# The bias behind the first norm moves from GpSimd to TensorE, and the step lists are laid out anew

## The chip, the cores and the metric

The kernel runs on one core of a Trainium2 chip. The metric is the device time of one execution in microseconds (us), the median of three runs. Five engines work side by side, each through its own list of instructions, and meet at semaphores: TensorE (PE in the profile; its weight loads are shown as PEld), VectorE (DVE), ScalarE (ACT), GpSimd (POOL) and SyncE (SP), which only issues transfers.

## The reference, cut to what matters

Input x is 16 batches of 512 tokens with 256 features. After a layer norm two branches run: an attention block with its own feed-forward layer, and a feed-forward layer with blockwise FP4 rounding, whose SiLU gates the first. The change sits in the attention block, behind the attention itself:

```
h   = _ln(x + attn_out, ln1_g, ln1_b)
ffn = gelu(h @ ffn_w1 + ffn_b1) @ ffn_w2 + ffn_b2
s   = _ln(h + ffn, ln2_g, ln2_b)
out = x0 + s * silu(fp4_ffn(x))
```

So the sum that enters the second norm is (x + attn_out, normed) * ln1_g + ln1_b + ffn_b2 + gelu(...) @ ffn_w2. The two rows ln1_b and ffn_b2 (256 numbers each) are the same for every token.

## The kernel before

Tokens lie on the 128 partitions, four groups of 128 tokens to a batch (T = 4). One batch is worked at a time, but its work is staggered: while the attention of batch b runs (`sc` scores, `pv` products with the values, `mx` row maxima for the other half batch, `proj` and `v` projections of batch b + 1, and the FP4 layer `gu`, `tr`, `dn`), the feed-forward part of batch b - 1 runs too (`cT`, `out`, `hT`, `f1`, `f2`, and the norms `ln1`, `ln2`). All this is cut into some 150 to 200 steps, and the order in which each of the five engines takes its steps is written out by hand in the table `ORDER`: a part `head` (setup and batch 0), a part `mid` that is repeated for batches 1 to 14, and a part `end` (batch 15 and the feed-forward part that is left over, `tail`). In `head` and `end` a step has its stretch in front (`pre:`, `pro:`, `first:`, `last:`, `tail:`). The engines do not reorder anything: a step that waits holds up all that stands behind it on its engine.

PSUM banks are given out in the order of TensorE's steps: banks 0 and 1 to `sc`, 6 and 7 in turn to `xT`, `proj`, `v`, `mx` and `mT`, and 2 to 5 in turn to all others. A step that reuses a bank waits for the engine that read it last, so a `mx` step waits for VectorE to be done with the `mx` step two before.

Steps that the change touches or that the prediction speaks of:

- `f2.t` on TensorE (L774 to L782): the second layer of the feed-forward part for 128 tokens, eight float32 products of 256 columns summed in one bank. In the trace each float32 product is two MATMUL rows (L781), a bfloat16 product is one.
- `f2.t` on VectorE (L1180 to L1183) adds the bank to `y2`.
- `lnb1` on GpSimd (L1273 to L1280): `y2 = hY * ln1_g`, then `y2 = y2 + (ffn_b2 + ln1_b)`, each 128x1024 per batch, in the tail in halves of 128x512. VectorE's `f2.t` waits for the second (event `g_hb2`).
- `xnb` on GpSimd (L1234 to L1246): xn + out_b, which VectorE's `out` adds; in batch 0 it first makes the sum of the two bias rows (L1238). SyncE's `xload` (L480 to L483) fetches the next batch into `xn` only when it is done (event `g_xnb`), and VectorE's `norm` of that batch waits for the load.
- `mul` on GpSimd (L1212), the elementwise product of the past score blocks, three instructions per head pair; `hq` and `hr`, the FP4 rounding of the gate branch (L1256, L1262, L1264); `tr` on TensorE (L723) waits for the last of them.
- in the setup, `wm` on GpSimd (L1440, L1442), `ws` and `wr` on VectorE (L1514 to L1528): FP4 rounding of the three weight matrices; `ws.2` needs the load `c2` (L1391, in_w_down). `soft` (L1572 to L1577) is the last step of the kernel-mask setup.
- `busy` on TensorE (L1672): products of no use in the setup.

Of the kernel before, what the change touches and what calls it, by code (L numbers as in the profile page):

```python
# [56 lines left out]
class Event:  # L57
# [5 lines left out]
    def wait(self, eng, b, k=None):  # L63

        if isinstance(b, int) and b < 0:
# [17 lines left out]
            pre:half pre:rs.0 pre:rs.1 pre:ones pre:iota pre:rs.2 pre:wm.0.0 pro:projm.0 pro:projm.1 pre:rs.3 pre:rs.4  # L83
            pro:projm.2 pre:rs.5 pre:rs.6 pre:rs.7 pre:rs.8 pre:rs.9 pre:rs.10 pre:wm.0.1 pre:rs.11 pre:rs.12 pre:wm.1.0
            pre:rs.13 pre:rs.14 pre:rs.15 pre:wm.1.1 pro:xq first:xnb pre:wm.2.0 pro:xr pre:wm.2.1 first:projm.0
            first:xq first:projm.1 first:projm.2 first:xr first:mul.0 first:mul.1 first:hq.0 first:mul.2 first:hr.0
# [16 lines left out]
            first:mx.1.3.0 first:muld.0.1 first:mx.1.3.1 first:silu.0.0 first:silu.0.1 first:mx.1.3.2 first:muld.1.0
            first:mx.1.3.3 first:hq.0 first:muld.1.1 first:v.0 first:mx.1.3.4 first:muld.2.0 first:mfin.1 first:v.1
            first:muld.2.1 first:hr.0 pre:pad first:silu.1.0 first:muld.3.0 first:muld.3.1 first:silu.1.1 first:silu.2.0
            pre:join first:muld.4.0 first:hq.1 first:muld.4.1 first:silu.2.1 first:hq.2 first:muld.5.0 first:hr.1
            first:muld.5.1 first:ctxt.0 first:mx.0.0.0 first:ctxt.1 first:mx.0.0.1 first:muld.6.0 first:dn.0
            first:mx.0.0.2 first:mx.0.0.3 first:mx.0.0.4 first:muld.6.1 first:silu.3.0 first:hr.2 first:silu.3.1
            first:mx.0.1.0 first:muld.7.0 first:mx.0.1.1 first:mx.0.1.2 first:mx.0.1.3 first:mx.0.1.4 first:muld.7.1
            first:hq.3 first:mx.0.2.0 first:mx.0.2.1 first:mx.0.2.2 first:mx.0.2.3 first:dn.1 first:mx.0.2.4  # L110
            first:mx.0.3.0 first:hr.3 first:mx.0.3.1 first:mx.0.3.2 first:ctxt.2 first:mx.0.3.3 first:mx.0.3.4
            first:dn.2 first:mfin.0 first:ctxt.3 first:dn.3
        """,
        tensor="""
            pre:arg.0 pre:arg.1 pre:arg.2 pre:arg.3 pre:sum.0 pre:arg.4 pre:arg.5 pre:arg.6 pre:sum.1 pre:sum.2
            pre:arg.7 pro:xT.0 pre:arg.8 pro:xT.1 pre:arg.9 pro:proj.0 pro:proj.1 pre:arg.10 pro:proj.2 pre:sum.3
            pre:sum.4 pre:arg.11 pro:v.0 pre:busy.0 pre:sum.5 pre:arg.12 pro:v.1 pre:sum.6 pre:sum.7 pre:busy.1
            pre:busy.2 pre:busy.3 pre:sum.8 pre:arg.13 pro:mx.0.0.0 pre:busy.4 pre:busy.5 pro:mx.0.0.1 pro:mx.0.0.2
            pre:sum.9 pro:mx.0.0.3 pro:mx.0.0.4 pro:mx.0.1.0 pre:sum.10 pre:busy.6 pro:mx.0.1.1 pro:mx.0.1.2 pre:sum.11
            pre:busy.7 pro:mx.0.1.3 pro:mx.0.1.4 pre:busy.8 pre:busy.9 pre:sum.12 pro:mx.0.2.0 pro:mx.0.2.1 pre:busy.10  # L120
            pre:busy.11 pre:busy.12 pre:busy.13 pro:mx.0.2.2 pre:busy.14 pro:mx.0.2.3 pre:busy.15 pro:mx.0.2.4
            pre:busy.16 pro:mx.0.3.0 pre:busy.17 pro:mx.0.3.1 pro:mx.0.3.2 pre:busy.18 pre:sum.13 pro:mx.0.3.3
            pre:sum.14 pro:mx.0.3.4 pre:sum.15 pre:sum.16 pre:busy.19 pre:sum.17 pre:poolT first:mx.1.0.0 pre:arg.14
            pre:mod first:mx.1.0.1 pre:gl pre:stat first:mx.1.0.2 first:mx.1.0.3 pro:mT.0 pre:arg.15 first:mx.1.0.4
            pre:busy.20 pre:wide first:mx.1.1.0 first:mx.1.1.1 pre:wt.0 first:mx.1.1.2 pre:kern pre:busy.21 pre:wt.1
            pre:wt.2 first:xT.0 pre:wt.3 first:xT.1 pre:wt.4 first:mx.1.1.3 pre:wt.5 pre:wt.6 first:mx.1.1.4 pre:wt.7
# [1678 lines left out]
```

## Time and profile before

| | us |
|---|---|
| median of three runs (1857.62 to 1858.73) | 1857.88 |
| the profiled execution, its own time | 1861.0 |
| its span, first to last instruction | 1859.2 |
| TensorE busy in the span | 1799.9 (97%) |
| VectorE, GpSimd, ScalarE busy | 1504.4 (81%), 1214.8 (65%), 1022.1 (55%) |
| mean granted TensorE clock | 0.991 |

Busy time is the time in which an engine has at least one instruction under way. TensorE's matmuls are pipelined: the mean length of one (380 ns for 256 float32 columns) is longer than the distance from its start to the next one's start, and it is that distance which counts when an engine is full.

### The profile page before, as it was taken

How to read it: one execution, taken by the hardware profiler on the slowest of the kernel's cores; microseconds unless marked ns; L12 is line 12 of the kernel's file. 1: busy time of each engine (PE TensorE's matmuls, PEld its weight loads, DVE VectorE, ACT ScalarE, POOL GpSimd, SP SyncE). 2: the span in 40 equal slices, each digit the busy share in tenths (PEclk: the TensorE clock that was granted, in tenths of full speed). 3: DMA queues.
4: the chain of work that ended last, by engine and by line, in shares of the span. 5: the costliest groups of instructions: out<-in, count | busy, mean ns of one | idle time of the engine just before them, and what ended most of it. 6: DMA issues, size and time to landing. Idle time of an engine off the chain costs nothing.

```text
span 1859.2 us, 37329 instructions
## 1 busy us (share of the span) xinstructions
PE 1799.9 (97%) x12687; PEld 1299.1 (70%) x12693; DVE 1504.4 (81%) x4977; ACT 1022.1 (55%) x2062; POOL 1214.8 (65%) x843
## 2 busy tenths in 40 slices
PE   8978999999999999999999999999999999999997
PEld 3335677777777777777777777777777777777766
DVE  6888889787888978788888978788897878888762
ACT  5535464655647465554736565564746555473642
POOL 3345677666758667675867767675875767586573
PEclk9989999999999999999999999999999999999999
DMA  6614242333323233333314233332323333331211
GB/s 189 200 43 109 56 140 79 100 113 89 114 80 106 74 102 116 96 102 100 113 52 139 80 100 110 93 113 70 113 78 100 113 93 109 100 112 49 65 59 35
DMA packets 146791, 181.44 MB, mean 98 GB/s; under 512 B 20605, under 2 KB 101630, under 8 KB 146596
## 3 DMA queue, kind: packets, MB, share of 16 engines
q1 hardware_dynamic: 146602, 179.05, 32.8%
q8 instruction: 103, 1.69, 0.4%
q14 instruction: 86, 0.70, 0.1%
HBM read 142.53 MB, written 36.47 MB: 96 GB/s over the span
## 4 chain that ended last, share of the span: by engine, by line
PE 58%; issue 20%; DVE 16%; POOL 4%; ACT 1%; DMA 1%; POOLq 0%; DVEq 0%; SPq 0%; ACTq 0%
PE ps L772 12%; PE ps L781 12%; PE ps L713 9%; PE ps L686 4%; PE ps L636 4%; PE ps L606 3%; PE ps L670 3%; PE ps L623 3%; DVE nmax L1068 2%; PE ps L666 2%; DVE Pr L1098 2%; DVE ps L1068 2%; POOL slot L1262 1%; PE ps L1598 1%; DVE y L1003 1%
## 5 line engine op out<-in xcount | busy, mean ns | idle before, releaser
L1068 DVE CUSTOM_DVE_ANT_0 ps<-ps,future 128x512 f32<-128x512 f32 (+3 forms) x1024 | 476.9, 516 | 62.6 <-issue 60.3
L1212 POOL TENSOR_TENSOR Pr<-Pr,Tz 128x768 f32<-128x768 f32 (+2 forms) x384 | 481.8, 1283 | 66.8 <-ACT Pr L854 65.4
L854 ACT ACTIVATE Pr<-ps 128x384 f32<-128x384 f32 x512 | 242.9, 487 | 210.3 <-PE ps L670 207.5
L772 PE MATMUL ps<-catT,w 128*128 128x256 f32 x1024 | 242.2, 382 | 1.1 <-ACT catT L919 1.1
L636 PE MATMUL ps<-KS,QS 108*128 108x512 bf16 (+3 forms) x1024 | 223.3, 301 | 10.7 <-DVE nmax L1068 4.1
L781 PE MATMUL ps<-w,gT 128*128 128x256 f32 x1024 | 232.3, 380 | 0.9 <-ACT gT L944 0.9
L781 PEld LDWEIGHTS ps<-w,gT 128*128 128x128 f32 x1024 | 190.8, 190 | 25.6 <-ACT gT L944 1.3
L772 PEld LDWEIGHTS ps<-catT,w 128*128 128x128 f32 x1024 | 188.4, 190 | 27.7 <-ACT catT L919 1.3
L1098 DVE SCALAR_TENSOR_TENSOR Pr<-ps,Tz 128x512 f32<-128x512 f32 x256 | 176.1, 688 | 31.5 <-ACT ps L843 26.3
L1272 POOL TENSOR_TENSOR rstd<-ve,minus_half 128x4 f32<-128x4 f32 (+1 forms) x34 | 33.5, 986 | 243.5 <-DVE ve L997 243.5
L1262 POOL TENSOR_TENSOR slot<-slot 128x704 f32<-128x704 f32 x64 | 107.6, 1681 | 120.5 <-DVE slot L972 120.5
L843 ACT ACTIVATE ps<-ps 128x512 f32<-128x512 f32 x256 | 150.5, 588 | 61.9 <-PE ps L666 61.6
L730 PE MATMUL ps<-wdT,hqT 128*128 128x256 f32 x768 | 178.8, 382 | 0.0
L713 PE MATMUL ps<-wgT,xqT 128*128 128x352 f32 x512 | 175.3, 465 | 1.1 <-ACT xqT L874 1.1
L713 PE MATMUL ps<-wuT,xqT 128*128 128x352 f32 x512 | 173.8, 462 | 0.0
L670 PE MATMUL ps<-QS,KS 112*128 112x384 bf16 (+2 forms) x768 | 160.6, 273 | 7.2 <-DVE Pr L1098 3.6
L730 PEld LDWEIGHTS ps<-wdT,hqT 128*128 128x128 f32 x768 | 141.6, 190 | 20.3 <-ACT hqT L893 2.3
L686 PE MATMUL ps<-Pr,v_cur 128*17 128x128 f32 (+2 forms) x3584 | 151.1, 319 | 0.0
L636 PEld LDWEIGHTS ps<-KS,QS 108*128 108x128 bf16 x1024 | 88.7, 98 | 87.7 <-DVE nmax L1068 30.6
L1068 DVE DVE_READ_ACCUMULATOR2_ANT nmax<- 128x1 f32 x1024 | 144.2, 141 | 0.0
L713 PEld LDWEIGHTS ps<-wuT,xqT 128*128 128x128 f32 x512 | 96.1, 190 | 58.7 <-ACT gT L944 7.4
L1256 POOL TENSOR_TENSOR slot<-slot,sc_h 128x704 f32<-128x704 f32 x64 | 95.5, 1492 | 59.8 <-PE ps L723 37.0
(251 smaller groups left out, 3351.2 us busy)
## 6 DMA issues: line engine op xcount, KB each, us to landing
Tz<-kernel_rows SPq DMA_DIRECT2D x256, 256.0 KB, 3.8
KS<-k_parts SPq DMA_DIRECT2D x32, 384.0 KB
QS<-q_parts SPq DMA_DIRECT2D x64, 192.0 KB
hY<-in_x SPq DMA_DIRECT2D x19, 512.0 KB, 5.2
xn<-in_x SPq DMA_DIRECT2D x17, 512.0 KB, 5.2
out<-y SPq DMA_DIRECT2D x15, 512.0 KB, 3.0
xnT<-in_x_t SPq DMA_DIRECT2D x14, 512.0 KB, 6.7
q_parts<-q_sp SPq DMA_DIRECT2D x16, 384.0 KB, 2.9
```

What stands on the lines that cost most here:

```text
L636: ins = mm(o, QS[0:KROWS, 2 * p + e, it * P:(it + 1) * P], KS[0:KROWS, p, 0:n], start=True, stop=True)
L670: ins = mm(dst[:, at:at + PAST[j]], KS[0:SROWS, p, j * P:(j + 1) * P], rhs[:, S - 1:P * (j + 1) - 1:-1], start=True, stop=True)
L686: ins = mm(dst[32 * hh:32 * hh + HD + 1, to:to + n], v_cur[:, j, 4 * g + hh, :], rhs[:, n - 1::-1], start=i == 0, stop=i == len(pieces) - 1)
L713: ins = mm(dst[:, 0:IH], xqT[:, c, t * P:(t + 1) * P], wt[:, c, f * IH:(f + 1) * IH], start=c == 0, stop=c == KD - 1)
L730: ins = mm(dst[:, 0:D], hqT[:, c * P:(c + 1) * P], wdT[:, c, :], start=c == 0, stop=c == KI - 1)
L772: ins = mm(dst[:, i * n:(i + 1) * n], w1[:, c, f * P:(f + 1) * P], catT[:, c, hf * n:(hf + 1) * n], start=c == 0, stop=c == KD - 1)
L781: ins = mm(dst[:, 0:D], gT[:, f, at:at + P], w2[:, f, :], start=f == 0, stop=f == KF - 1)
L843: inc(af(src, src, ACT.Exp), "a_exp")
L854: inc(af(Pr[:, p % 4, e, at:at + wd], src[:, 0:wd], ACT.Exp), "a_exp")
L1068: ins = v.tensor_tensor_reduce(o, o, future[:, S - n:S], -1.0, 3e38, ALU.add, ALU.min, nmax[:, 2 * pl + e, it:it + 1])
L1098: v.scalar_tensor_tensor(blocks(Pr[:, p % 4, e, 0:S]), blocks(ps[:, SC_BANKS[n % len(SC_BANKS)], :]), 3e38, near, ALU.min, ALU.mult).then_ ...
L1212: ins = g.tensor_tensor(a, a, Tz[:, p % 2, :, P * j:P * j + PAST[j]], ALU.mult)
```

## The change

Two things are done. First, GpSimd's second instruction of `lnb1` goes (the addition of `ffn_b2 + ln1_b` to all tokens), with the event `g_hg` between the two. In its place every `f2.t` step on TensorE gets a ninth product into the same bank: 96 rows deep, 128 wide, 256 columns, bfloat16. Its stationary side `bias_pick` is zero but for rows 0, 32 and 64, which are one; its moving side `bias_rows` holds in these rows the bias row cut into three bfloat16 parts, high, middle and low, whose sum is the float32 row. Both lie in the tile of `ln1_b`, no longer needed as such. The parts are made once, by ten more GpSimd instructions ahead of the first `xnb`.

Second, the table `ORDER` is laid out anew for all five engines in all three parts. The lines that compute, cut to the core (of `ORDER`, one line as an example):

```diff
-            ln1 mul.0 lnb1 xnb mul.1 hq.0 xt mul.2 hr.0 projm.0 hq.1 projm.1 mul.3 projm.2 hr.1 xq mul.4 hq.2 hr.2 mul.5
+            ln1 mul.0 xnb lnb1 mul.1 hq.0 xt mul.2 hr.0 hq.1 projm.0 mul.3 projm.1 projm.2 hr.1 xq mul.4 hq.2 hr.2 mul.5
...
+        bias_split = row["ln1_b"][:].bitcast(BF16)
+        bias_rows, bias_pick = bias_split[0:96, 0:D], bias_split[0:96, D:D + P]
...
                     for f in range(KF):
                         at = (t % 2) * P
-                        ins = mm(dst[:, 0:D], gT[:, f, at:at + P], w2[:, f, :], start=f == 0, stop=f == KF - 1)
-                    inc(ins, "pe_f2")
+                        mm(dst[:, 0:D], gT[:, f, at:at + P], w2[:, f, :], start=f == 0, stop=False)
+                    if b == 1 and t == 0:
+                        pe.wait_ge(L["row_sum"], 11)
+                    inc(mm(dst[:, 0:D], bias_pick, bias_rows, start=False, stop=True), "pe_f2")
...
                         pool.wait_ge(L["row_sum"], 1)
+                        r = row["ffn_b2"]
+                        g.memset(bias_pick, 0.0).then_inc(L["row_sum"], 1)
+                        pool.wait_ge(L["row_sum"], 2)
+                        for i in range(3):
+                            g.memset(bias_pick[32 * i:32 * i + 1, :], 1.0).then_inc(L["row_sum"], 1)
+                            pool.wait_ge(L["row_sum"], 3 + i)
+                        g.tensor_copy(bias_rows, r[0:96]).then_inc(L["row_sum"], 1)
+                        pool.wait_ge(L["row_sum"], 6)
+                        g.tensor_tensor(r[0:96], r[0:96], bias_rows, ALU.subtract).then_inc(L["row_sum"], 1)
+                        pool.wait_ge(L["row_sum"], 7)
+                        for i in (1, 2):
+                            g.tensor_copy(bias_rows[32 * i:32 * i + 32, :], r[32 * i:32 * i + 32]).then_inc(L["row_sum"], 1)
+                            pool.wait_ge(L["row_sum"], 7 + i)
+                        g.tensor_tensor(r[64:96], r[64:96], bias_rows[64:96, :], ALU.subtract).then_inc(L["row_sum"], 1)
+                        pool.wait_ge(L["row_sum"], 10)
+                        g.tensor_copy(bias_rows[64:96, :], r[64:96]).then_inc(L["row_sum"], 1)
+                        pool.wait_ge(L["row_sum"], 11)
...
-                    inc(g.tensor_tensor(y2[:, tt, :], hY[:, tt, :], wide("ln1_g"), ALU.mult), "g_hg")
-                    E["g_hg"].wait(pool, b - 1, hf)
-                    inc(g.tensor_tensor(y2[:, tt, :], y2[:, tt, :], wide("ffn_b2"), ALU.add), "g_hb2")
+                    inc(g.tensor_tensor(y2[:, tt, :], hY[:, tt, :], wide("ln1_g"), ALU.mult), "g_hb2")
```

Three places of the lists, each before and after. In these rows a tile that is written stands left of the arrow; `ps` is PSUM.

TensorE in a batch of the repeated part, around the first `f2` step, before:

```order
L670 MATMUL ps<-QS,KS 128x384
L636 MATMUL ps<-KS,QS 128x256 x2
L781 MATMUL ps<-w,gT 128x256 x8
L670 MATMUL ps<-QS,KS 128x256
L670 MATMUL ps<-QS,KS 128x128
L666 MATMUL ps<-QS,KS 128x128 x4
L644 MATMUL ps<-ident_bf,sh_sp 16x128 x4
L606 MATMUL ps<-xnT,cq 128x512 x2
```

The same place after the change (lines are three to six numbers further down; L784 is the old L781, L787 the new product, which names only the one tile that holds both its operands):

```order
L673 MATMUL ps<-QS,KS 128x384
L639 MATMUL ps<-KS,QS 128x256 x2
L784 MATMUL ps<-w,gT 128x256 x8
L787 MATMUL ps<-row_ln_b 128x256
L673 MATMUL ps<-QS,KS 128x256
L673 MATMUL ps<-QS,KS 128x128
L669 MATMUL ps<-QS,KS 128x128 x4
L647 MATMUL ps<-ident_bf,sh_sp 16x128 x4
L609 MATMUL ps<-xnT,cq 128x512 x2
```

The steps here stand in the same order; each `f2` has one bfloat16 product of 256 columns more.

GpSimd in the setup, from the bias row's sum to the rounding of the third weight matrix, before (L1238 makes the sum, L1245 is `xnb`, L1442, L1440 and L1442 are `wm.2`):

```order
L1238 TENSOR_TENSOR row_ffn_b<-row_ffn_b,row_ln_b 128x256 [waits pro_w_rest,pro_stat]
L1245 TENSOR_TENSOR xnb<-xn,row_out_b 128x1024 [waits v_norm,pro_row_sum]
L1442 TENSOR_TENSOR gT<-gT,gs_old 128x1536 [waits pro_wq]
L1227 TENSOR_TENSOR catT<-catT,sc_x 128x1024 [waits v_xq]
L1440 TENSOR_TENSOR gT<-gT,slot 128x768 [waits pro_wq]
L1440 TENSOR_TENSOR gT<-gT,hqT 128x768
L1442 TENSOR_TENSOR gT<-gT,gs_old 128x1536 [waits pro_wpool]
```

and after:

```order
L1243 TENSOR_TENSOR row_ffn_b<-row_ffn_b,row_ln_b 128x256 [waits pro_w_rest,pro_stat]
L1246 MEMSET row_ln_b 96x128 [waits pro_row_sum]
L1249 MEMSET row_ln_b 1x128 [waits pro_row_sum] x3
L1251 CAST row_ln_b<-row_ffn_b 96x256 [waits pro_row_sum]
L1253 TENSOR_TENSOR row_ffn_b<-row_ffn_b,row_ln_b 96x256 [waits pro_row_sum]
L1256 CAST row_ln_b<-row_ffn_b 32x256 [waits pro_row_sum] x2
L1258 TENSOR_TENSOR row_ffn_b<-row_ffn_b,row_ln_b 32x256 [waits pro_row_sum]
L1260 CAST row_ln_b<-row_ffn_b 32x256 [waits pro_row_sum]
L1267 TENSOR_TENSOR xnb<-xn,row_out_b 128x1024 [waits v_norm,pro_row_sum]
L1462 TENSOR_TENSOR gT<-gT,gs_old 128x1536 [waits pro_wq]
L1460 TENSOR_TENSOR gT<-gT,slot 128x768 [waits pro_wq]
L1460 TENSOR_TENSOR gT<-gT,hqT 128x768
```

Ten small instructions (the rows with x3 and x2 counted as such) stand between the sum and `xnb`, and the second scaling of the rounded input (L1227) no longer stands between the two parts of `wm.2`.

SyncE in the setup, from the last load of the weights to the first transfer of the masks' shifts, before:

```order
L1391 DMA gT<-in_w_down 128x2x704
L1403 DMA stat_rows<-xnb 64x128 [waits pro_statc]
L1403 DMA stat_rows<-xnb 64x128
L483 DMA xn<-in_x 128x4x256 [waits g_xnb,g_xs]
L537 DMA shift_parts<-sh_T 16x512 [waits a_mT]
L543 DMA QS<-shift_parts 2x4x512 [waits d_shw0]
L543 DMA QS<-shift_parts 2x4x512
```

and after:

```order
L1423 DMA stat_rows<-xnb 64x128 [waits pro_statc]
L1423 DMA stat_rows<-xnb 64x128
L540 DMA shift_parts<-sh_T 16x512 [waits a_mT]
L546 DMA QS<-shift_parts 2x4x512 [waits d_shw0]
L546 DMA QS<-shift_parts 2x4x512
L1411 DMA gT<-in_w_down 128x2x704
L486 DMA xn<-in_x 128x4x256 [waits g_xnb,g_xs]
```

The load of `in_w_down` stood ahead of two waits and now stands behind three, and the load of `xn` behind it.

## Rows read from the trace of the kernel before

**Rows 1.** The page, part 1: busy us, share of the span, instructions.

```profile
PE 1799.9 (97%) x12687; PEld 1299.1 (70%) x12693; DVE 1504.4 (81%) x4977; ACT 1022.1 (55%) x2062; POOL 1214.8 (65%) x843
```

**Rows 2.** Windows: stretch, its length, then busy us, instructions by engine, clock, DMA.

```profile
100.00:150.00 50.00, 34.34 (x184) 17.18 (x185) 45.26 (x112) 21.15 (x55) 19.13 (x9) 0.80 0.11 21
329.04:1712.33 1383.29, 1373.56 (x9987) 1021.69 (x9985) 1150.29 (x3823) 786.15 (x1535) 953.72 (x651) 1.00 0.33 98
```

**Rows 3.** Timeline, TensorE in one batch: start us, us, engine, line, what, count.

```profile
1005.75 0.33 PE L670 MATMUL ps<-QS,KS 112*128 112x256 bf16 x2
1005.92 0.60 PE L694 MATMUL ps<-ident,ctxT 128*128 128x128 f32 x4
...
1007.38 3.62 PE L781 MATMUL ps<-w,gT 128*128 128x256 f32 x16
1010.83 0.33 PE L670 MATMUL ps<-QS,KS 112*128 112x256 bf16 x2
```

**Rows 4.** Timeline, TensorE in the setup, where the rows in use change.

```profile
96.88 0.39 PE L636 MATMUL ps<-KS,QS 108*128 108x512 bf16 x1
97.20 1.12 PE L1611 MATMUL ps<-ctxT,Tz 6*128 6x512 f32 x2
98.25 0.62 PE L1629 MATMUL ps<-pooledT,gs 128*128 128x16 f32 x4
```

**Rows 5.** Timeline over one batch's seam, TensorE.

```profile
1181.05 0.38 PE L636 MATMUL ps<-KS,QS 108*128 108x256 bf16 x2
1181.71 0.88 PE L723 MATMUL ps<-ident,slot 128*128 128x128 f32 x6 [0.28 <-POOL slot L1264]
...
1193.11 0.33 PE L670 MATMUL ps<-QS,KS 112*128 112x256 bf16 x2
1193.45 0.40 PE L666 MATMUL ps<-QS,KS 112*128 112x128 bf16 x4
1194.02 0.34 PE L670 MATMUL ps<-QS,KS 112*128 112x384 bf16 x1 [0.18 <-ACT Pr L854]
```

**Rows 6.** Lines by form: count, busy us, mean ns, idle us ahead.

```profile
L1280 POOL TENSOR_TENSOR y<-y,row_ffn_b 128x1024 f32<-128x1024 f32 x15 | 35.4, 2357 | 1.2
```

**Rows 7.** Timeline, GpSimd in the setup.

```profile
13.09 0.24 POOL L1419 MEMSET ident_bf<- 128x128 bf16 x1
...
110.05 0.98 POOL L1238 TENSOR_TENSOR row_ffn_b<-row_ffn_b,row_ln_b 128x256 f32<-128x256 f32 x1 [7.51 <-DMA stat_rows<-xnb]
111.11 3.21 POOL L1245 TENSOR_TENSOR xnb<-xn,row_out_b 128x1024 f32<-128x1024 f32 x1
121.45 2.81 POOL L1442 TENSOR_TENSOR gT<-gT,gs_old 128x1536 f32<-128x1536 f32 x1 [7.13 <-DVE gs_old L1519]
```

**Rows 8.** Timeline, SyncE and VectorE in the setup.

```profile
114.39 0.38 SPq L483 DMA_DIRECT2D xn<-in_x  x1
114.82 0.50 SPq L537 DMA_DIRECT2D shift_parts<-sh_T  x1
118.47 1.42 SPq L543 DMA_DIRECT2D QS<-shift_parts  x2
...
118.11 1.75 DVE L1514 TENSOR_REDUCE gs_old<-gT 128x96 f32<-128x1536 f32 x1
125.30 1.22 DVE L972 TENSOR_TENSOR catT<-catT,hY 128x1024 f32<-128x1024 f32 x1
```

**Rows 9.** DMA issues between 60 and 150 us: KB each, us to landing.

```profile
gT<-in_w_down SPq DMA_DIRECT2D x1, 704.0 KB, 9.1
xn<-in_x SPq DMA_DIRECT2D x1, 512.0 KB, 3.7
```

**Rows 10.** The chain in the last batch (first row); timeline of the tail.

```profile
1729.23 0.96 ACT gs_old L905
...
1824.58 1.27 POOL L1280 TENSOR_TENSOR y<-y,row_ffn_b 128x512 f32<-128x512 f32 x1
1833.70 0.42 DVE L1183 TENSOR_TENSOR y<-ps,y 128x256 f32<-128x256 f32 x1 [9.92 <-PE ps L781]
```

More of the change, by code:

```diff
@@ L82 @@
         gpsimd="""
[L83 to L86, printed above, removed]
+            pre:half pre:iota pre:rs.0 pre:rs.1 pre:rs.2 pre:wm.0.0 pro:projm.0 pre:rs.3 pro:projm.1 pre:rs.4
+            pro:projm.2 pre:ones pre:rs.5 pre:rs.6 pre:rs.7 pre:rs.8 pre:rs.9 pre:rs.10 pre:wm.0.1 pre:rs.11 pre:rs.12
+            pre:wm.1.0 pre:rs.13 pre:rs.14 pre:rs.15 pre:wm.1.1 pro:xq first:xnb pre:wm.2.0 pre:wm.2.1 pro:xr first:xq
+            first:projm.0 first:projm.1 first:xr first:projm.2 first:mul.0 first:mul.1 first:hq.0 first:mul.2 first:hr.0
             first:mul.3 first:hq.1 first:mul.4 first:hr.1 first:hq.2 first:mul.5 first:hr.2 first:mul.6 first:hq.3
@@ L103 @@
[L103 to L112, printed above, removed]
+            pre:modT first:mx.1.0.0 first:mx.1.0.1 pre:fr.14 pre:peak first:mx.1.0.2 first:mx.1.0.3 pre:topk
@@ new lines @@
+            first:mx.1.0.4 first:mx.1.1.0 pre:fr.15 pre:kw first:mx.1.1.1 first:mx.1.1.2 pro:xr pre:ws.2 pro:xr2
+            first:norm pre:wr.2 pre:soft first:mx.1.1.3 first:mx.1.1.4 pre:join first:xq first:mx.1.2.0 first:proj.0
+            first:mx.1.2.1 first:proj.1 first:xr first:proj.2 first:mx.1.2.2 first:xr2 first:muld.0.0 first:mx.1.2.3
+            first:mx.1.2.4 first:mx.1.3.0 first:muld.0.1 first:mx.1.3.1 first:silu.0.0 first:muld.1.0 first:silu.0.1
+            first:mx.1.3.2 first:mx.1.3.3 first:hq.0 first:muld.1.1 first:mx.1.3.4 first:silu.1.0 first:v.0
@@ L117 @@
[L117 to L126, printed above, removed]
@@ new lines @@
+            pre:busy.11 pro:mx.0.2.1 pro:mx.0.2.2 pre:busy.12 pre:busy.13 pro:mx.0.2.3 pre:busy.14 pro:mx.0.2.4
+            pre:busy.15 pro:mx.0.3.0 pro:mx.0.3.1 pre:busy.16 pre:busy.17 pre:busy.18 pro:mx.0.3.2 pro:mx.0.3.3
+            pre:sum.13 pre:sum.14 pre:sum.15 pro:mx.0.3.4 pre:sum.16 pre:sum.17 first:mx.1.0.0 first:mx.1.0.1 pre:arg.14
+            pre:stat pre:busy.19 pre:poolT pre:arg.15 pre:mod pre:gl first:mx.1.0.2 first:mx.1.0.3 pro:mT.0
+            first:mx.1.0.4 pre:busy.20 first:mx.1.1.0 pre:wide first:mx.1.1.1 first:mx.1.1.2 pre:kern pre:wt.0
@@ L161 @@
+            first:dn.2 first:tr.3.0 first:tr.3.1 first:mT.0 first:dn.3
         """,
@@ L204 @@
         sync="""
-            last:T.0 last:load.1 last:T.1 last:T.2 last:T.3 last:mio.1 last:T.4 last:T.5 last:T.6 last:T.7 last:fin
+            last:T.0 last:load.1 last:T.1 last:T.2 last:T.3 last:T.4 last:mio.1 last:T.5 last:T.6 last:T.7 last:fin
             tail:xr tail:fin.0 tail:fin.1
@@ L208 @@
         gpsimd="""
-            last:ln1 last:hq.0 last:mul.0 last:hr.0 last:mul.1 last:hq.1 last:lnb1 last:mul.2 last:xnb last:hr.1
-            last:mul.3 last:hq.2 last:mul.4 last:hr.2 last:mul.5 last:hq.3 last:hr.3 last:mul.6 last:mul.7 last:ln2
-            last:fin tail:ln1.0 tail:ln1.1 tail:lnb1.0 tail:lnb1.1 tail:ln2.0 tail:fin.0 tail:ln2.1 tail:fin.1
+            last:ln1 last:hq.0 last:mul.0 last:hr.0 last:xnb last:mul.1 last:lnb1 last:mul.2 last:hq.1 last:mul.3
+            last:hr.1 last:hq.2 last:mul.4 last:hr.2 last:mul.5 last:hq.3 last:hr.3 last:mul.6 last:mul.7 last:ln2
@@ L223 @@
-            tail:ln1.1 tail:lnc1.1 last:dn.3 tail:f2.0 tail:f2.1 tail:ln2.0 tail:lnc2.0 tail:lnb2.0 tail:f2.2 tail:f2.3
-            tail:ln2.1 tail:lnc2.1 tail:lnb2.1
+            last:silu.0.0 last:out.0 last:out.1 last:muld.0.0 last:ln1 last:silu.0.1 last:muld.0.1 last:lnc1 last:hq.0
+            last:silu.1.0 last:muld.1.0 last:mx.1.0.0 last:mx.1.0.1 last:mx.1.0.2 last:muld.1.1 last:silu.1.1
+            last:mx.1.0.3 last:hr.0 last:mx.1.0.4 last:mx.1.1.0 last:mx.1.1.1 last:muld.2.0 last:mx.1.1.2 last:muld.2.1
@@ L256 @@
+            tail:f1.1.0 tail:f1.1.1 tail:f1.1.2 tail:f1.1.3
         """,
```

222 lines of the change are left out of this document (115 added, 107 removed).

## Prediction

> **What bounds the kernel.** I read the page's busy times first: TensorE is busy for 97% of the span, GpSimd, which the change relieves, for 65% [rows 1]. A mean over stages proves little, so the windows come next. From the first transposes of batch 1's rounded tokens to those of batch 14 (thirteen equal stretches, 106.4 us each) TensorE is busy for 1373.6 of 1383.3 us, VectorE for 83%, GpSimd for 69%; the setup from 100 to 150 us is another matter, there VectorE is busy for 45.3 of 50 us and TensorE for 34.3, at a clock of 0.80 [rows 2]. In the repeated part, then, whatever is added to TensorE lengthens the batch, and whatever is taken from GpSimd is worth only what TensorE waits because of it. In the setup it is the other way round.
>
> Busy time hides short waits, since the ends of matmuls are modelled. So I read the timeline start to start. The 16 rows of one `f2` go from 1007.38 to 1010.83, 0.216 us each [rows 3], with no room between. At a seam between batches I find real waits: the two 256-column products at 1181.05 need 0.22 us, but the next step starts 0.66 us later, a wait of 0.44 us for the last rounding on GpSimd (`tr.3.0`); at 1193.11 and 1193.45 a step of 0.16 and one of 0.22 us are followed at 0.34 and 0.57 us, another 0.53 us, for ScalarE's exponentials [rows 5]. Going through one batch in this way I count about 2.2 us of such waits, in ten places. They recur alike in each batch. That is all that a new order could give back in a batch.
>
> **The change, part by part.**
>
> *The ninth product.* Four `f2` steps per batch, 16 batches: 64 products of 256 bfloat16 columns. The nearest rows: a 256- and a 128-column bfloat16 product together take 0.17 us (1005.75 to 1005.92) [rows 3], so two thirds, 0.11 us, for 256 columns. Those use 112 of the array's rows, this one 96. It stands behind float32 products of 128 rows and 128 columns, as the `sc` steps often do, and the trace shows no loss there: behind the `f2` at 1007.38 the next row starts on time. 64 x 0.11 = 7.0 us. Ends: 128 columns' worth, 0.055 us each, 3.5 us; and 0.11 plus a loss at the change of shape on both sides, 0.30 us each, 19 us (second rival). I take 7.0, and all of it on the path, since the waits listed above hang on TensorE's own progress: `mx` steps wait for VectorE to finish a `mx` that TensorE has delivered just before, `tr.3.0` for a chain that starts behind `dn.1`. None stands behind an `f2` and could swallow its lengthening.
>
> *GpSimd's addition.* 15 of 2.357 us [rows 6] and two halves of 1.27 us in the tail [rows 10], 37.9 us of GpSimd's time. Who waits for it? VectorE's `f2`, which in the tail starts at 1833.70, when the last addition has been done since 1825.85 [rows 10]; in a batch the distance is larger. What stands behind it on GpSimd is `xnb` and `mul.1`. They come 2.4 us sooner, but the next point where TensorE waits for GpSimd is `tr.3.0`, 80 us further on, and there GpSimd itself waited before it for VectorE's rounding `hr.3`. So the gain is nothing; at the other end, if all of the 0.44 us went in 14 batches, 6 us.
>
> *The new order of the repeated part.* I laid the two lists side by side at each of the ten waits. For `sc.0.3` and `sc.0.4` ScalarE's copy `vcopy` has been moved from ahead of `sc.0.1` to ahead of `cT`; but `sc.0.4` reuses the bank of `sc.0.2`, which TensorE delivers at 1193.44 (1193.11 and its own 0.33) and ScalarE then reads; it started at 1194.02 [rows 5], and can't start much sooner in either order. In the first quarter `mx.1.1.0` gets its bank some 0.15 us sooner, but `f1.0.0` behind it waits for ScalarE's `hT` as before. From `dn.1` on, where four of the waits lie (0.06 to 0.45 us), TensorE's steps are the same. In the third quarter the `mx` steps are pulled forward by one, which lets VectorE start sooner but also brings each closer to the one whose bank it takes; by my sums they keep 0.1 to 0.9 us in hand. So I take 0 for the 14 batches, with 0.3 us per batch either way, 4 us.
>
> *The setup.* Ten small GpSimd instructions stand between the bias sum and `xnb`. Bounds: 0.24 us, as a memset of 128x128, and 0.98 us, as an addition of 128x256 [rows 7]. Four memsets near the first and six others at 0.5 to 1.0 us, with some 0.1 us between them: 5 to 8 us, I take 6.3. Behind `xnb` (ended 114.3) GpSimd was idle for 7.13 us, until VectorE had the scales of the third weight matrix [rows 7]; this covers it, barely. But `xload` also waits for `xnb`: it was issued at 114.39 and takes 3.7 us [rows 8, 9]; 6.3 us later it lands at 124.4. VectorE wanted it behind the scales, which GpSimd took up at 121.45 [rows 7]. In the new order the two roundings `xr2`, two instructions of 1.22 us [rows 8], stand ahead of it, so it is wanted at 123.9: 0.5 us late, less what the statistics arrive sooner. Further, the load of `in_w_down` stood ahead of everything, and now stands behind the shifts' transfers. The first of them landed 3.65 us after it was issued (114.82 to 118.47) [rows 8]; from a start near 108.5, my estimate from the order of ScalarE's steps, and with 1.4 us for the next two [rows 8], the weight load is issued at about 113.6. It took 9.1 us when many loads were under way [rows 9]; alone, scaled from 512 KB in 3.7 us [rows 9], 5.1 us, so it lands at 118.7 to 122.7, and VectorE wants it at 118.11 [rows 8]. VectorE has no idle time from there on. I take 0.6 us for this and 0.1 for `xload`; with the rest of the setup's new order, of which I can work out little, the bounds are -4 and +5 us.
>
> *The last batch.* ScalarE's copy `gs_old`, 0.96 us [rows 10], no longer stands directly ahead of the normalization that TensorE's `hT` waits for; an exponential of 0.48 us takes its place. I take -0.5 us.
>
> *Sum.* 7.0 + 0 + 0 + 0.7 - 0.5 = 7.2 us. The profiled execution took 1861.0 us, of which 1.8 us lie around the span of 1859.2 us; it becomes 1868.2. The median of the runs is 3.1 us lower than that execution, and the same sum on it gives 1857.9 + 7.2 = 1865.1 us.
>
> **The rivals.**
>
> *The waits go (the other side).* With GpSimd and VectorE less pressed, the new order could meet the banks in time: if half of the 2.2 us per batch goes, 14 x 1.1 = 15 us, against 7: 1850 us. For it speaks that all lists have been laid out anew around the lighter GpSimd; against it, that the waits I looked up are set by TensorE's own step and the one reader behind it, in both orders. It wins from 0.6 us per batch on.
>
> *A loss at each ninth product.* Where the rows in use change from 108 to 6 and back to 128, the trace shows losses: the 512-column product at 96.88 is followed after 0.32 instead of 0.22 us, and the two at 97.20 take 1.05 instead of 0.86 us [rows 4], so about 0.1 us each way. If 96 rows counted as a change of shape, 0.19 us x 64 = 12 us more, 1877 us. Against it: 108, 112 and 128 rows alternate everywhere without loss. 
>
> *The setup loses.* The weight load lands late by its long duration (4.6 us), and the small instructions take 8 us, so `xload` is late by 2: about 5 us more than I take, 1870 us.
>
> *The order gives a little.* Some 0.25 us per batch in 14 batches, 3.5 us: 1861.5 us.
>
> A second rule of the skill bears on the product's price: "TensorE: Matmul & The Clock Gate", Back-to-back issue gap, gives some 81 ns for 128 and 131 ns for 512 columns in a stream of weight loads and matmuls. By it, read between the two, 64 products would cost about 6 us. The rows of this kernel disagree for 512 columns (0.22 us), and the sum goes by them.
>
> **How the numbers follow.** Forecast 60%; the order gives a little 15%; the setup loses 10%; the waits go 10%; a loss at each product 5%. The range from 1859 to 1871 takes in the forecast with its own bounds (the 4 us of the order and the setup's, not both at their ends), the setup's loss and most of the small gain. A difference of 0.2%, 3.7 us, is about what a measurement of this kernel can tell from none: 1854.2 to 1861.6. Faster than that: 9%, nearly all from the first rival. Within: 16%, from half of the small gain and the forecast's lower edge. Slower: 75%.
>
> **What would show it.** In the profile after: 64 more bfloat16 matmuls of 96 rows, followed by the next row after 0.11 us; a batch of 106.8 us instead of 106.4; 38 us less on GpSimd, and longer idle stretches there. The wait of 0.44 us at `tr.3.0` and the 0.53 us at `sc.0.3` and `sc.0.4` are still there. In the setup, VectorE's fourth norm step behind `xr2` at about 124 us. I am wrong in the step on the order if a batch takes 106.4 us or less, in the price of the product if it takes 107.2 or more, and in the setup if batch 1 starts more than 3 us earlier or later than the sum says.

## The result, and the profile after

| | before | changed |
|---|---|---|
| median, us (5 runs each) | 1858.33 (1857.62 to 1860.96) | 1866.13 (1865.23 to 1869.89) |
| the profiled execution, its span | 1861.0, 1859.2 | 1869.89, 1868.1 |

The ratio is 1.0038, 95% interval 1.0027 to 1.0048: 7.1 us slower (5.0 to 8.9). The forecast was 1865.1 us. The profiled execution of the changed kernel is the longest of its five, so the profiled pair shows 8.9 us; 1.8 of these lie ahead of the repeated batches, nearly all in the setup, and I come back to them.

The page, part 1, of the changed kernel: TensorE has its 64 matmuls more than in [rows 1], GpSimd loses 12.8 us where I had said 38.

```profile
PE 1811.4 (97%) x12751; PEld 1307.4 (70%) x12757; DVE 1513.1 (81%) x4977; ACT 1017.8 (54%) x2064; POOL 1202.0 (64%) x836
```

Two windows of the changed kernel, columns as in [rows 2]: the thirteen repeated batches between the same two instructions as there, and what follows. These two are the first transposes of the rounded tokens of batch 2 and of batch 15, counted from 0 as in the lists; the prediction calls them batch 1's and batch 14's, and what it calls the start of batch 1 is the transposes of batch 0 (`pro:xqT`). No sum hangs on that.

```profile
330.82:1719.81 1388.99, 1378.49 (x10038) 1026.60 (x10037) 1155.51 (x3823) 779.49 (x1535) 939.73 (x638) 1.00 0.34 98
1719.81:1868.10 148.29, 132.65 (x890) 103.88 (x888) 82.12 (x250) 70.00 (x140) 71.78 (x54) 0.99 0.17 50
```

1388.99 against 1383.29 us [rows 2] is 5.70 us, or 13 x 4 x 0.11 us. From start to start, TensorE's timeline of one `f2` shows where they are: the ninth product (L787) starts at 1122.46, the next row at 1122.58.

```profile
1122.46 0.27 PE L787 MATMUL ps<-row_ln_b 96*128 96x256 bf16 x1
1122.58 0.33 PE L673 MATMUL ps<-QS,KS 112*128 112x256 bf16 x2
```

The seam between batches 9 and 10 answers to [rows 5]. The two `mx` products at 1186.73 are followed after 0.67 us (0.66 before); `sc.0.3` at 1198.97 is followed after 0.74 us where its four products take 0.22, so 0.52 us of waiting (0.53 before).

```profile
1186.73 0.38 PE L639 MATMUL ps<-KS,QS 108*128 108x256 bf16 x2
1187.40 0.87 PE L726 MATMUL ps<-ident,slot 128*128 128x128 f32 x6 [0.29 <-POOL slot L1286]
...
1198.80 0.33 PE L673 MATMUL ps<-QS,KS 112*128 112x256 bf16 x2
1198.97 0.39 PE L669 MATMUL ps<-QS,KS 112*128 112x128 bf16 x4
1199.71 0.34 PE L673 MATMUL ps<-QS,KS 112*128 112x384 bf16 x1 [0.36 <-ACT Pr L859]
```

So far the trace says: product at its price, order nothing. The experiments show that the second half of this is true only of the two together.

### The profile page after: what moved, and what is told of

It reads as the page before. It is cut to its first block, busy times and chain, and to the rows that moved or that the text cites. A ratio compares the mean times of both kernels' runs of the same rounds, so it can differ in the third digit from the quotient of the medians.

```text
span 1868.1 us, 37450 instructions
## 1 busy us (share of the span) xinstructions
PE 1811.4 (97%) x12751; PEld 1307.4 (70%) x12757; DVE 1513.1 (81%) x4977; ACT 1017.8 (54%) x2064; POOL 1202.0 (64%) x836
## 4 chain that ended last, share of the span: by engine, by line
PE 55%; issue 21%; DVE 18%; POOL 4%; ACT 1%; DMA 0%; POOLq 0%; DVEq 0%; SPq 0%; ACTq 0%
PE ps L775 11%; PE ps L784 11%; PE ps L716 9%; PE ps L639 4%; PE ps L689 4%; PE ps L609 3%; PE ps L673 3%; DVE nmax L1073 2%; PE ps L669 2%; DVE Pr L1103 2%; DVE ps L1073 2%; PE ps L626 1%; POOL slot L1284 1%; DVE y L1008 1%; DVE y L1016 1%
## 5 line engine op out<-in xcount | busy, mean ns | idle before, releaser
L784 PE MATMUL ps<-w,gT 128*128 128x256 f32 x1024 | 233.1, 381 | 0.9 <-ACT gT L949 0.9
L784 PEld LDWEIGHTS ps<-w,gT 128*128 128x128 f32 x1024 | 190.3, 190 | 26.4 <-ACT gT L949 1.3
L1278 POOL TENSOR_TENSOR slot<-slot,sc_h 128x704 f32<-128x704 f32 x64 | 101.3, 1583 | 78.3 <-DVE sc_h L966 47.0
```

What stands on the lines that cost most here:

```text
L784: mm(dst[:, 0:D], gT[:, f, at:at + P], w2[:, f, :], start=f == 0, stop=False)
```

## The experiments

Each kernel was timed in turns with the kernel before, whose median was then 1859.9 to 1860.7 us, some 2 us higher than above; so ratios are compared, not times. "Batch" is the median distance between the thirteen repeated batches in the one profiled execution: 106.34 us in the kernel before, 106.78 in the changed one. The mean is 0.1 us or less above it, but for three kernels that are named below.

### The product alone, the lists alone

Edit of the first: all three parts of `ORDER` as before, the rest as changed. Edit of the second: the other way round.

> The changed code with the step lists of the kernel before in all three parts: the ninth products alone. Theory (product at the price of its 256 rows, 64 x 0.11 us, nothing hidden; the lists pay about 1 us of their own in the setup): 1858.3 + 7.0 = 1865.3 us, that is 0.8 us under the changed kernel. Rival A (the lists carry the loss, the product hides in waits): near 1859 to 1861. Rival B (the new lists win something in the repeated batches and the product costs more than 0.11 us): above 1867, and the repeated batch over 106.85 us. Repeated batch by the theory: 106.34 + 0.44 = 106.78 us.

Measured: 1867.89 us against 1860.67, ratio 1.0036 (1.0023 to 1.0048), batch 106.79 us. The same as the changed kernel. Rival A falls by the time, and rival B by the batch, which is under its 106.85 us.

> The code of the kernel before (GpSimd adds the bias, eight products) with the new step lists in all three parts: the new order alone. Theory: 0 in the repeated batches (106.34 us each) and +1 to +2 us at the setup and the last batch: 1859.3 to 1860.3. Rival A (the order itself costs most of the 7.8 us): 1864 or more. Rival B (the order gives something that the product hides): under 1857.5, with a repeated batch under 106.2 us.

Measured: 1883.73 us, ratio 1.0118 (1.0103 to 1.0134). The theory is far off, the change in parts does not add up: product +6.7 us, lists +22, both together +7.1. The batch takes 107.84 us. Two of VectorE's rows, grouped by line, say where to look. They are the addition of epsilon to the variances (128x4 values, four on each partition), in this kernel and then in the changed one:

```profile
L998 DVE TENSOR_SCALAR ve<-mv 128x4 f32<-128x4 f32 (+1 forms) x34 | 25.6, 752 | 1.2
```

```profile
L1002 DVE TENSOR_SCALAR ve<-mv 128x4 f32<-128x4 f32 (+1 forms) x34 | 6.5, 192 | 1.2
```

### The ninth product left out, and issued twice

```diff
-                    inc(mm(dst[:, 0:D], bias_pick, bias_rows, start=False, stop=True), "pe_f2")
+                    inc(ins, "pe_f2")        # ins: the eighth product, with stop=True
```

> The changed kernel with its ninth product left out (the sum ends at the eighth f32 product, so the two biases are missing from the second layer); everything else as changed, the part rows are still made in the setup. Theory: 64 x 0.11 = 7.0 us less than the changed kernel, 1859.1 us, and it agrees with the kernel that has the new lists alone. Rival A (a wait moves into the gap): less than 4 us less, 1862 or more. Rival B (a shape change of 0.19 us at each product as well): 12 us or more less, under 1855.

Measured: 1883.27 us, ratio 1.0115 (1.0100 to 1.0130), batch 107.84. Taking 64 products out of the changed kernel makes it 14 us slower. It agrees with the kernel that has the lists alone, as expected, but both are on the far side of what any of the theories allowed. The timeline of one batch of this kernel, VectorE, GpSimd and then TensorE, shows the mechanism:

```profile
1274.61 1.63 DVE L1002 TENSOR_SCALAR ve<-mv 128x4 f32<-128x4 f32 x1
1276.16 0.56 DVE L1073 CUSTOM_DVE_ANT_0 ps<-ps,future 128x384 f32<-128x384 f32 x1
```

```profile
1274.40 1.81 POOL L1217 TENSOR_TENSOR Pr<-Pr,Tz 128x768 f32<-128x768 f32 x1 [0.29 <-ACT Pr L859]
```

```profile
1277.07 0.39 PE L639 MATMUL ps<-KS,QS 108*128 108x512 bf16 x1 [0.24 <-DVE nmax L1073]
1278.50 0.67 PE L626 MATMUL ps<-vw,xnT 128*128 128x256 f32 x2 [1.04 <-DVE nmax L1073]
```

GpSimd's product starts at 1274.40 and ends at 1276.21. VectorE's addition of 128x4 values starts at 1274.61, 0.20 us behind it, and ends at 1276.24, with it. It lasts 1.63 us; the next maxima are late by as much, and TensorE waits for them at `v.1`. In the changed kernel the same two instructions stand so:

```profile
1266.11 0.17 DVE L1002 TENSOR_SCALAR ve<-mv 128x4 f32<-128x4 f32 x1
```

```profile
1266.12 1.82 POOL L1217 TENSOR_TENSOR Pr<-Pr,Tz 128x768 f32<-128x768 f32 x1 [0.51 <-ACT Pr L859]
```

VectorE is ahead by 15 ns, and not held. In its thirteen repeated batches the lead is 4 to 15 ns, in the kernel without the product VectorE is behind by 193 to 207 ns, in the kernel before ahead by some 400. Between 4 ns ahead and 193 ns behind lies 1.5 us per batch. Where exactly the edge lies the runs do not show: one addition that the trace puts 2 ns behind (in the kernel with the setup's old lists, further down) was not held. The four products of a batch shift the two instructions by 0.2 us against each other with the old lists too: with the product alone the lead is 0.65 us. The Trainium skill's "SBUF — State Buffer", section "Who interferes with whom", has the rule: VectorE and GpSimd share one pair of ports, an exclusive lock for a whole instruction, taken by whichever issues first, and `tensor_scalar` is among the operations that can need it. This trace agrees: in the repeated batches the addition is held to within 0.03 us of the end of GpSimd's instruction where it is behind, and not where it is ahead.

> The changed kernel with the ninth product issued twice in each sum (the biases are added twice): 64 more bf16 products of the same kind, back to back with the first. Theory: each costs its 0.11 us again, 7.0 us more than the changed kernel: 1873.1 us, batch 107.22 us. Rival A (the first one pays for a change of type that the second does not): clearly less than what leaving out the first gives back. Rival B (products are partly covered by the waits of the batch): less than 4 us more.

Measured: 1873.85 us, ratio 1.0075 (1.0063 to 1.0088), against 1.0038 a further 0.37% or 6.9 us. Batch 107.2 us, 0.43 more; the second product starts 0.11 us behind the first. VectorE's lead grows to some 240 ns. The price is linear but for one of the thirteen batches. That one took 112.3 us, 5.1 more than the others (the mean is 107.6), and it shows how dear the edge is: a copy of 128x4 values starts 0.03 us behind GpSimd's product and lasts 1.80 us, the addition behind it is held as well, and TensorE waits twice for the maxima, 1.89 and 1.04 us. After these waits the clock granted to TensorE was 0.57 in the mean from 1057 to 1061 us, so for most of it at the lower of its two levels (1.2 instead of 2.4 GHz), and the eight rows of `v.1` took 3.31 us from start to start instead of 1.73. VectorE, GpSimd, then TensorE:

```profile
1052.45 1.80 DVE L998 COPY ve<-st 128x4 f32<-128x4 f32 x1
1054.57 0.90 DVE L1003 TENSOR_SCALAR ve<-mv 128x4 f32<-128x4 f32 x1
```

```profile
1052.42 3.71 POOL L1218 TENSOR_TENSOR Pr<-Pr,Tz 128x768 f32<-128x768 f32 x3
```

```profile
1056.31 0.39 PE L639 MATMUL ps<-KS,QS 108*128 108x512 bf16 x1 [1.89 <-DVE nmax L1074]
1057.74 3.48 PE L626 MATMUL ps<-vw,xnT 128*128 128x256 f32 x8 [1.04 <-DVE nmax L1074]
```

Why VectorE came late in that one batch I did not trace.

### The lists alone, without the collision

```diff
-        mv = sb("mv", [P, T, 2])
+        mv = sb("mv", [P, T, 3])                   # column 2 holds EPS
...
-                inc(v.tensor_scalar(ve[:, tt], mv[:, tt, 1], EPS, None, ALU.add), "v_ve")
+                inc(v.tensor_reduce(ve[:, tt], mv[:, tt, 1:3], AX.X, ALU.add), "v_ve")
```

> As the kernel with the new lists alone, but the one VectorE operation that was held there by GpSimd (the addition of the epsilon on 128x4 values, 1.63 us in the repeated batches against 0.17 us in the changed kernel) is a reduction over two columns instead, the second a constant column of epsilon; same place in the list, same values. Theory (the new lists put this operation 0.2 us behind the start of a 1.81 us GpSimd product, they share a port into SBUF, and the wait of 1.2 us of TensorE at v.1 is that): the operation takes about 0.2 us again, the wait at v.1 goes, batch 106.4 us or less instead of 107.84, total 1883.7 - 15 x 1.45 = 1862 us, range 1859 to 1864. Rival (the lists lose the 1.5 us by the order of the steps itself, the long operation only shows idle time): the batch stays above 107.5 us and the total above 1880.

Measured: 1864.00 us against 1860.49, ratio 1.0022 (1.0013 to 1.0030), batch 106.39. By the ratio that is 18 us less than with the scalar addition, and its time is the upper edge of what was expected. The two instructions stand as unluckily as before, VectorE's 0.20 us behind, and it takes 0.16 us:

```profile
1259.11 0.16 DVE L998 TENSOR_REDUCE ve<-mv 128x4 f32<-128x8 f32 x1
```

```profile
1258.91 1.82 POOL L1213 TENSOR_TENSOR Pr<-Pr,Tz 128x768 f32<-128x768 f32 x1 [0.28 <-ACT Pr L855]
```

That settles what costs the 1.5 us per batch: the held addition, since the order of the steps is the same in both kernels. That a shared port is what holds it is the page's account; the runs show who is held and for how long. The same page of the Trainium skill says of `tensor_reduce` on this chip that it never contends; the rows agree. What stays are 4 us by the ratio, and in the profiled execution 3.1 lie behind the repeated part (149.96 us from the window's end to the end, against 146.87). The kernel with the lists alone has the same (149.7); without GpSimd's addition and without the product it is 147.4. So the new order of the last batch loses some 2.5 us when GpSimd still has its addition to make, and fits the changed code only. Each is a figure of one execution.

> The changed kernel with the epsilon added by the two-column reduction instead of the scalar addition, as in the lists-alone kernel that lost its long operation. Theory (in the changed kernel this addition starts just ahead of GpSimd's product and is not held, 192 ns in the mean): nothing to remove, 1866.1 us within 2 us, batch 106.78 us. Rival (some of the change's loss is also such a collision): 1862 or less.

The same edit on the changed kernel. Measured: ratio 1.0045 (1.0032 to 1.0057), batch 106.77. Nothing to gain there, as expected.

### The product with 32 rows

```diff
-                    inc(mm(dst[:, 0:D], bias_pick, bias_rows, start=False, stop=True), "pe_f2")
+                    inc(mm(dst[:, 0:D], bias_pick[0:32], bias_rows[0:32], start=False, stop=True), "pe_f2")
```

> The changed kernel with only the first 32 rows in the ninth product (the high part of the bias alone; middle and low parts are left out). Theory: 32 rows lie behind a product of 128 rows as another shape of the array and lose what other products of 32 or 16 rows lose there, some 0.09 to 0.19 us each: 64 x 0.14 = 6 to 12 us more, 1872 to 1878 us. Rival (only the number of columns sets the price): 1866 us, a ninth product followed after 0.11 us as before.

Measured: 1882.18 us (2 runs), ratio 1.0120 (1.0100 to 1.0139), batch 107.63; the rival falls, and the time is above the theory's range. TensorE's timeline around one of them:

```profile
1233.15 0.59 PE L784 MATMUL ps<-w,gT 128*128 128x256 f32 x2
1233.68 0.28 PE L787 MATMUL ps<-row_ln_b 32*128 32x256 bf16 x1
1233.89 0.34 PE L673 MATMUL ps<-QS,KS 112*128 112x256 bf16 x2
```

The last row of the `f2` starts at 1233.37 (two rows from 1233.15, 0.22 apart) and is followed after 0.31 instead of 0.22 us; the ninth is followed after 0.21 instead of 0.11. So 0.2 us are lost on the two sides together, as [rows 4] had it, where the theory took 0.14, and 96 rows count as no change of shape.

### The setup's lists

> The changed kernel with the setup's lists of the kernel before (pre, pro, first), the lists of the repeated batches and of the end as changed. Theory (of the change's loss 1 to 2 us is the setup's, since TensorE takes two maxima, arg.14 and stat ahead of the pooled chain): 1 to 2 us under the changed kernel, 1864.5 us, and the setup's end (first transposes of batch 1) at 149.4 us instead of 151.3. Rival (the setup's difference is only that of one execution): the same as the changed kernel, 1866.

Measured: 1870.96 us, ratio 1.0060 (1.0046 to 1.0074): if anything worse than the changed kernel, and not better. The theory falls. The start of batch 0's transposes, which the expectation calls batch 1's, says nothing either way. It is at 147.50 us here and was at 151.31 in the changed kernel's profile, but in kernels with the very same setup lists it is at 147.58 (product twice), 148.25 and 151.66. With the lists of before I find 146.93 to 150.39. More than half of that spread is there by the first `proj.0`, which I did not trace further. Changed kernel, then the kernel with the product twice, TensorE:

```profile
28.72 1.98 PE L609 MATMUL ps<-xnT,cq 128*128 128x512 f32 x4
...
151.31 0.74 PE L708 MATMUL ps<-ident,catT 128*128 128x128 f32 x5 [0.43 <-issue]
```

```profile
26.66 1.98 PE L609 MATMUL ps<-xnT,cq 128*128 128x512 f32 x4
...
147.58 0.63 PE L708 MATMUL ps<-ident,catT 128*128 128x128 f32 x4 [0.53 <-issue]
```

So the 1.8 us of the profiled pair can't be put down to the change. Why this mixture is 0.2% slower than either whole set stays open; its profiled execution is the fastest of its six (1866.80 to 1872.93 us), so the trace shows nothing of it.

### Can the waits of the kernel before be filled?

Four attempts at a kernel faster than both, all on the kernel before. The first is on TensorE:

```diff
-            ... sc.0.3 sc.0.4 gu.0.1 sc.0.5 sc.1.0 mx.1.0.0 mx.1.0.1 gu.1.0
+            ... sc.0.3 gu.0.1 sc.0.4 sc.0.5 mx.1.0.0 mx.1.0.1 sc.1.0 gu.1.0
```

> The kernel before with one move in TensorE's repeated list: gu.0.1 stands ahead of sc.0.4 instead of behind it, and sc.1.0 behind mx.1.0.1, so that the two banks of sc are free by the time. Theory: the 0.17 + 0.34 us in which TensorE waits for ScalarE's exponentials at sc.0.3 and sc.0.4 mostly go: at least 0.3 us of them, batch 106.0 us, total 1858.3 - 15 x 0.35 = 1853 us (1850 to 1856). Rival A (another wait takes their place, because silu.0.1 and the steps behind it on ScalarE are no earlier): batch 106.34, same time. Rival B (VectorE's chain gets later by a collision with GpSimd): slower, 1860 or more.

Measured: 1861.06 us, ratio 1.0004 (0.9996 to 1.0013), batch 106.43: rival A. TensorE now waits at `sc.0.5` for VectorE's product, which stands behind the statistics of the norm:

```profile
1197.09 0.33 PE L671 MATMUL ps<-QS,KS 112*128 112x384 bf16 x1
1197.64 0.34 PE L671 MATMUL ps<-QS,KS 112*128 112x256 bf16 x2 [0.23 <-DVE Pr L1099]
```

> The kernel before with gu.0.1 ahead of sc.0.4 on TensorE as in the run that tried only that, and mx.1.0.0 and mx.1.0.1 between sc.0.4 and sc.0.5, so that the product which frees sc.0.5's bank (VectorE's, behind the norm's statistics) is done by then. Theory (that run lost its 0.34 us again by 0.23 us at sc.0.5 and 0.07 us at pv.0): the wait at sc.0.4 goes and none takes its place, batch 106.1 us, 1858.3 - 15 x 0.25 = 1854.5 us. Rival (the later softmax steps or maxima take it up again): 106.3 to 106.5 us a batch, no change that can be measured.

Measured: 1864.23 us, ratio 1.0020 (1.0012 to 1.0029), batch 106.43 (the mean is 106.54, with two long batches). The rival by the batch, but the whole is 3.7 us longer, clear of noise, of which the profile shows less than 2 in the repeated batches; the rest stays open. One wait, of 0.6 us, stands at `mx.1.0.0`, where the profile names a transfer as what ended it, and one of 0.4 us at `pv.0`.

```profile
1196.80 0.61 PE L637 MATMUL ps<-KS,QS 108*128 108x512 bf16 x3 [0.46 <-DMA QS<-q_bias_parts]
...
1212.92 1.35 PE L687 MATMUL ps<-Pr,v_cur 128*17 128x384 f32 x17 [0.24 <-ACT gT L945]
```

Then comes the other wait, `tr.3.0`: VectorE makes the subtraction of `hr.3`.

```diff
-                    fp4_round(hs[t % 2][:, 0:I], mbuf[t % 2], "v_hq", b, 3 * t + 2, False)
+                    fp4_round(hs[t % 2][:, 0:I], mbuf[t % 2], "v_hq", b, 3 * t + 2, t == 3)
```

> The kernel before with the subtraction of the last rounding of a batch (hr.3, 1.68 us on GpSimd) made by VectorE (0.89 us), so that the rounded rows are ready earlier for tr.3.0. Theory (TensorE's 0.45 us at tr.3.0 ends with GpSimd's last product): that wait goes nearly whole, batch 105.95 us, 1858.3 - 15 x 0.4 = 1852 us (1851 to 1856). Rival A (VectorE's 0.9 us there delay the maxima and the wait appears at mx.0.3.3 or in the next batch): 1858 within 1 us. Rival B (both): slower.

Measured: 1873.68 us, ratio 1.0073 (1.0061 to 1.0086), batch 107.15, 0.8 us longer: rival B. The wait at `tr.3.0` is gone (1191.24 to 1191.46), but VectorE's 0.89 us delay the maxima, and TensorE waits for these twice:

```profile
1186.39 2.36 PE L686 MATMUL ps<-Pr,v_cur 128*17 128x384 f32 x56
1189.36 0.39 PE L636 MATMUL ps<-KS,QS 108*128 108x512 bf16 x1 [0.60 <-DVE nmax L1068]
1190.13 0.39 PE L636 MATMUL ps<-KS,QS 108*128 108x384 bf16 x2 [0.38 <-DVE nmax L1068]
...
1191.24 0.38 PE L636 MATMUL ps<-KS,QS 108*128 108x256 bf16 x2
1191.46 0.82 PE L723 MATMUL ps<-ident,slot 128*128 128x128 f32 x6
```

> As the one before, and also TensorE's gu.0.1 ahead of sc.0.4 with VectorE's muld.0.1 ahead of ln1, so that the wait for the product of sc.0.3 does not take the place of the one at sc.0.4. Theory (the waits are apart and both can be filled): 0.3 us a batch more than by the subtraction alone, 1848 us. Rival (the norm comes 1.5 us later and hT waits for it): no better than the subtraction alone.

Measured: 1911.32 us, ratio 1.0279 (1.0265 to 1.0293), batch 109.5 (the mean is 109.8): far worse than even the rival. With the norm's steps 1.2 us later, another small VectorE instruction, the 128x4 `shift`, meets GpSimd's product, 0.06 us behind it, in every batch (VectorE, GpSimd, then TensorE):

```profile
1227.43 1.76 DVE L1179 SCALAR_TENSOR_TENSOR shift<-mv,rstd 128x4 f32<-128x4 f32 x1 [1.13 <-POOL rstd L1276]
```

```profile
1227.37 1.80 POOL L1213 TENSOR_TENSOR Pr<-Pr,Tz 128x768 f32<-128x768 f32 x1
```

```profile
1230.92 0.39 PE L637 MATMUL ps<-KS,QS 108*128 108x512 bf16 x1 [1.80 <-DVE nmax L1069]
```

It is held for 1.6 of the 2.3 us that the batch is longer than in the attempt before; no run here takes that one hold away. No version beats the kernel before.

## Why the prediction was right, point by point

- **The ninth product, 7.0 us.** Right in size and in place: 0.11 us from start to start, 5.70 us in thirteen batches; the product alone costs 0.36% or 6.7 us, a second one 6.9. The 19 us end of the range is the price of 32 rows, not of 96.
- **GpSimd's addition, nothing.** Right for the time: TensorE waits at `tr.3.0` as before, and the product alone, with the addition gone, costs the product's price. Wrong in the row: of the 37.9 us taken off, GpSimd shows 12.8. Some 5 went into the part rows, and some 20 into the same instructions at greater length; the rounding product of 128x704 values took 1492 ns in the mean and now 1583, the subtraction of 128x128 values (`projm.2`) 670 and now 992:

```profile
L1278 POOL TENSOR_TENSOR slot<-slot,sc_h 128x704 f32<-128x704 f32 x64 | 101.3, 1583 | 78.3 <-DVE sc_h L966 47.0 <-PE ps L726 31.0
...
L1209 POOL TENSOR_TENSOR bias_sp<-bias_r,bias_sp 128x128 bf16<-128x128 f32 x16 | 15.9, 992 | 1.4 <-ACT bias_sp L831 1.4
```

  The lists do that: with the product alone GpSimd's page row is 1179.9 us, 34.9 less than [rows 1]. The subtraction is held by VectorE: in both kernels it ends 0.29 us behind a VectorE instruction that was under way when it started, and that one now ends 0.36 us later. The batch does not show it: the 0.44 us more are the product's price.
- **The new order, 0 with 0.3 us per batch either way.** Right for this kernel, wrong as reasoning. I compared TensorE's list at each wait and took durations as fixed. The order alone loses 1.5 us per batch, five times my bound, because it moves a VectorE instruction across the start of a GpSimd instruction. That the changed kernel doesn't pay is due to the product, which shifts the two by 0.2 us against each other. I had named no term for that, and the forecast hung on 4 to 15 ns: that the 0 came out was luck. The trace of the kernel before had the sign in its last batch, where both small instructions of the norm are held beside a GpSimd product and take 1.60 and 0.93 us, against 0.17 us for the addition in the batches before:

```profile
1802.10 1.60 DVE L992 COPY ve<-st 128x4 f32<-128x4 f32 x1
...
1804.01 0.93 DVE L997 TENSOR_SCALAR ve<-mv 128x4 f32<-128x4 f32 x1
```

```profile
1801.86 3.74 POOL L1212 TENSOR_TENSOR Pr<-Pr,Tz 128x768 f32<-128x768 f32 x3
```

- **The setup, +0.7 us.** Not told apart. GpSimd's ten instructions took 5.1 us (I said 6.3); `in_w_down` was issued at 113.06 (113.6); GpSimd, then SyncE:

```profile
112.10 0.20 POOL L1246 MEMSET row_ln_b<- 96x128 bf16 x1
...
117.32 2.37 POOL L1267 TENSOR_TENSOR xnb<-xn,row_out_b 128x1024 f32<-128x1024 f32 x1
```

```profile
113.06 0.40 SPq L1411 DMA_DIRECT2D gT<-in_w_down  x1
...
119.77 0.38 SPq L486 DMA_DIRECT2D xn<-in_x  x1
```

  But the norm behind `xr2` came at 129.08, not at about 124: the second of the two 1.22 us subtractions lasted 3.71 us, VectorE first and then GpSimd,

```profile
124.19 1.23 DVE L977 TENSOR_TENSOR catT<-catT,hY 128x1024 f32<-128x1024 f32 x1
125.45 3.71 DVE L980 TENSOR_TENSOR catT<-catT,hY 128x1024 f32<-128x1024 f32 x1
129.08 1.05 DVE L1031 TENSOR_SCALAR xn<-xn,mean_all,rstd_all 128x256 f32<-128x256 f32 x3
```

```profile
124.23 3.85 POOL L1462 TENSOR_TENSOR gT<-gT,gs_old 128x1536 f32<-128x1536 f32 x1 [4.54 <-DVE gs_old L1539]
```

  beside a GpSimd product that ends at 128.08, 1.08 us before it; the first of the pair took 1.23 us here and 1.22 in the kernel before [rows 8]. The two engines hold each other in turn, as in the batches: VectorE's first subtraction starts 0.04 us ahead, and GpSimd's product takes 3.85 us against 2.81 [rows 7]; the second starts behind that product and is held. The forecast had no term for this here either. The whole is below what medians tell, since product alone and full change agree within 0.1%.
- **The last batch, -0.5 us.** 148.29 against 146.87 us in the profiled pair; with the product alone 147.8, and eight products are 0.9 of that. So the lists cost about 0.5 us, and the sign was wrong, as far as single executions tell.
- **The rivals.** The waits did not go in the change. In my four attempts those that I filled came back at other steps or cost more than they were. The loss at each ninth product is real for 32 rows, and not there for 96.

## What to carry to other kernels

A shift of 0.2 us between two engines that do not bound the kernel cost 1.5 us per batch here, because it carried a short VectorE instruction on SBUF data across the start of a long GpSimd one. List such pairs with their distance; where that is no larger than the shifts that the change makes, price both cases, or give the short one a form that isn't held (here a reduction). Undo the parts of a change one at a time: product and lists alone would have been judged +7 and +22 us, and together they are +7. In this kernel a wait on the full engine was not free time: each of the three that I filled came back at another step, or as a longer one.

## What the runs showed of the hardware

- A `tensor_scalar` over 128x4 values takes 0.17 us, and 1.63 us when it starts 0.2 us behind a GpSimd `tensor_tensor` of 1.81 us; a `scalar_tensor_tensor` with two SBUF inputs of that size 0.16 and 1.76 us; a `tensor_reduce` in the same place as the first 0.16 us; a copy of 128x4 values 1.80 us, 0.03 us behind three such GpSimd products. 4 ns ahead were enough not to be held. GpSimd is held as well when it is the one behind: 3.85 us instead of 2.81, 0.04 us behind a two-input VectorE subtraction.
- A bfloat16 product of 256 columns behind float32 products costs 0.11 us with 96 rows and 0.31 us with 32.
- The start of batch 0's transposes lay between 146.9 and 151.7 us in the profiled executions, and between 147.6 and 151.7 in kernels with the same setup lists.
